# Weighted values of an attention stage: the values as the loaded matrix in column tiles, the transposed weights moving

## The reference, cut to what matters

```python
q, k, v = split_heads(x @ Wq + bq), split_heads(x @ Wk + bk), split_heads(x @ Wv + bv)   # 16 heads of 8
scores = (q k^T + c2p + p2c) / sqrt(24)          # c2p, p2c: relative positions, gathered
probs = softmax(scores, axis=-1)
ctx = einsum('bhqk,bhkd->bhqd', probs, v)        # 128 x 128 weights by 128 x 8 values, per head and batch
out = ctx.reshape(B, S, H) @ Wo + bo + x         # then the layer norm, the outer residual, a second norm
```

## Time and profile before

| | before |
|---|---|
| median of three runs | 2927.15 us |
| profiled execution | 2934.35 us |
| its span | 2932.60 us |
| PE busy | 2580.1 us |
| ACT busy | 2331.3 us |
| DVE busy | 2220.2 us |
| mean granted clock of TensorE | 0.893 of full |

### The profile page before, as it was taken

The page is one execution under the profiler, slowest core; times in us unless marked ns, Lnnn a source line. Parts: engine busy times, 40 slices in busy tenths (PEclk is TensorE's granted clock), DMA queues, the critical chain, the costliest instruction groups (busy, mean ns, idle before and its releaser), DMA issues. The chain is left out here.

```text
span 2932.6 us, 63537 instructions
## 1 busy us (share of the span) xinstructions
PE 2580.1 (88%) x17943; PEld 1570.5 (54%) x17943; DVE 2220.2 (76%) x6591; ACT 2331.3 (79%) x4575; POOL 576.6 (20%) x436
## 2 busy tenths in 40 slices
PE   2999999999999934765669999999999999999997
PEld 1777777777777823652434444444444444444443
DVE  3667767777677657777558888888888888888887
ACT  1778877788788825332779999999999999999997
POOL 2222232222322200113421111111111111111114
PEclk7778978889788855988789999999999999999999
DMA  2000000000000010000011111111111111211113
GB/s 76 13 14 19 11 11 11 16 16 11 11 12 19 2 42 1 0 29 1 0 30 53 47 43 58 43 52 49 43 58 43 52 49 43 58 43 51 50 43 86
DMA packets 182538, 96.02 MB, mean 33 GB/s; under 512 B 22539, under 2 KB 179291, under 8 KB 182491
## 3 DMA queue, kind: packets, MB, share of 16 engines
q1 hardware_dynamic: 182491, 95.45, 11.6%
HBM read 78.10 MB, written 4.73 MB: 28 GB/s over the span
## 5 line engine op out<-in xcount | busy, mean ns | idle before, releaser
L1904 DVE TENSOR_TENSOR c_Hl<-c_HF,c_Hh 128x512 f16<-128x512 f32 x1028 | 679.7, 688 | 160.6 <-ACT c_Hh L1791 144.6
L1787 ACT ACTIVATE c_HF<-c_H,c_b 128x512 f32<-128x512 f32 x1028 | 710.3, 691 | 67.3 <-PE c_H L1726 44.5
L1791 ACT ACTIVATE c_Hh<-c_H,c_b 128x512 f16<-128x512 f32 x1028 | 705.3, 686 | 0.0
L1842 POOL TENSOR_TENSOR c_EX<-c_euler,c_D 128x16 f32<-128x16 f32 x65 | 188.6, 2901 | 1195.8 <-DVE c_D L1877 1195.8
L1726 PE MATMUL c_H<-c_Ch,SH 128*128 128x512 f16 x1028 | 390.0, 379 | 0.0
L1725 PE MATMUL c_H<-c_Cl,SH 128*128 128x512 f16 x1028 | 390.0, 379 | 0.0
L1724 PE MATMUL c_H<-c_Ch,SH 128*128 128x512 f16 x1028 | 390.0, 379 | 0.0
L1735 PE MATMUL c_Y<-c_Hh,SH 128*128 128x512 f16 x1024 | 388.0, 379 | 1.5 <-DVE c_Hl L1904 1.4
L1737 PE MATMUL c_Y<-c_Hl,SH 128*128 128x512 f16 x1024 | 388.1, 379 | 0.0
L1736 PE MATMUL c_Y<-c_Hh,SH 128*128 128x512 f16 x1024 | 388.1, 379 | 0.0
L554 ACT ACTIVATE a_E<-a_T,a_nm 128x128 f32<-128x128 f32 x1024 | 331.0, 417 | 33.0 <-DVE a_nm L642 30.9
(11 more groups left out here) (290 smaller groups left out, 4298.0 us busy)
## 6 DMA issues: line engine op xcount, KB each, us to landing
c_CWB<-c_rows SPq DMA_DIRECT2D x260, 256.0 KB, 4.1
a_QN<-a_QH SPq DMA_DIRECT2D x128, 32.0 KB, 1.8
a_KN<-a_KH SPq DMA_DIRECT2D x128, 32.0 KB, 1.8
out<-d_O SPq DMA_DIRECT2D x16, 256.0 KB, 2.3
a_QN<-a_QL SPq DMA_DIRECT2D x64, 32.0 KB, 1.8
a_KN<-a_KL SPq DMA_DIRECT2D x64, 32.0 KB, 1.8
CUR<-in_ctx SPq DMA_DIRECT2D x1, 1848.0 KB
c_rows<-c_CWR SPq DMA_DIRECT2D x65, 8.0 KB, 1.3
```

Of the source, the lines that this page charges most:

```text
L1787: act.activation(HF[:, k % 4, :], bH[k % 4][:, :], ACT.Gelu_apprx_tanh, bias=b1[:, g % EXPERTS, f:f + 1], scale=1.0 / WSCALE).then_inc(hf_ ...
L1791: act.activation(Hh[:, g % 2, f, :], bH[k % 4][:, :], ACT.Gelu_apprx_tanh, bias=b1[:, g % EXPERTS, f:f + 1], scale=1.0 / WSCALE).then_inc( ...
L1904: dve.tensor_tensor(Hl[:, g % 2, f, :], HF[:, k % 4, :], Hh[:, g % 2, f, :], ALU.subtract)\
```

## The change

The operands of the value product are exchanged. V is stored with 32 columns per head (VCOLS): eight values, a one, and zeros. It is the loaded matrix now, and the 128 queries of ET move. Each of the four heads of a unit writes its own 32 partitions of bO, and the unit its own 128 columns. The result is thus transposed: values on partitions, queries along the row.

To bring it back, ACT copies bO to a new tile OC (`unit_columns`, in steps 7, 11, 15, 19), and PE transposes OC unit by unit (`out_rows`, in steps 9, 13, 17, 21). These transposes go to the two banks bE as well. The banks are handed on by position in one sequence, SLOTS, in which the outputs of a batch come after unit 7, 11, 15 and at the end; slot n uses bank n % 2 and waits (`bank_free`) for the reader of slot n - 2. The steps of the reciprocal move from 7, 11, 15, 19 to 9, 13, 17, 21, those of `out_transpose` and `out_columns` to 10, 14, 18, 22, and those of `out_project` to 11, 15, 19, 23.

```diff
+VCOLS = 32
+def bank_slots():
+    out = []
+    for w in range(UNITS):
+        out.append(("unit", w))
+        if w >= UPB + 3 and w % UPB == 3:
+            out.append(("out", w // UPB - 1))
+    return out + [("out", NB - 1)]
...
-        V = sb("V", [P, NB, NH, DH + 1])
+        V = sb("V", [P, NB, NH, VCOLS])
+        OC = sb("OC", [P, UPB, S])
...
+            const(pool.memset(V[:, :, :, :], 0.0))
...
             def exp_transposes(i, w):
                 pe.wait_ge(e_ok.sem, e_ok.at(i, w + 1))
-                pe.wait_ge(et_ok.sem, et_ok.at(i, w - 1))
+                bank_free(i, slot_of(w))
                 for h in range(HG):
-                    last = pe.transpose(bE[w % 2][:, h * S:(h + 1) * S], E[:, w % 3, h, :], ident[:, :])
+                    last = pe.transpose(bE[slot_of(w) % 2][:, h * S:(h + 1) * S], E[:, w % 3, h, :], ident[:, :])
                 last.then_inc(et_ps.sem, 1)
+            def bank_free(i, slot):
+                kind, k = SLOTS[slot - 2]
+                if kind == "unit":
+                    pe.wait_ge(et_ok.sem, et_ok.at(i, k + 1 if slot >= 2 else 0))
+                else:
+                    pe.wait_ge(on_ok.sem, on_ok.at(i, k + 1 if slot >= 2 else 0))
+            def out_rows(i, b):
+                slot = SLOTS.index(("out", b))
+                pe.wait_ge(oc_ok.sem, oc_ok.at(i, b + 1))
+                bank_free(i, slot)
+                for g in range(UPB):
+                    last = pe.transpose(bE[slot % 2][:, g * S:(g + 1) * S], OC[:, g, :], ident[:, :])
+                last.then_inc(oc_ps.sem, 1)
...
                 if g == 0:
-                    pe.wait_ge(on_ok.sem, on_ok.at(i, b))
+                    pe.wait_ge(oc_ok.sem, oc_ok.at(i, b))
...
                 for h in range(HG):
-                    at = (g * HG + h) * (DH + 1)
-                    last = pe.matmul(bO[:, at:at + DH + 1], ET[:, w % 3, h, :], V[:, b, g * HG + h, :],
-                                     start=True, stop=True)
+                    last = pe.matmul(bO[VCOLS * h:VCOLS * (h + 1), g * S:(g + 1) * S], V[:, b, g * HG + h, :],
+                                     ET[:, w % 3, h, :], start=True, stop=True)
...
-                    if u >= 8 and (u - 8) % UPB == 0:
-                        out_transpose(i, (u - 8) // UPB, last)
-                    if u >= 9 and (u - 9) % UPB == 0:
-                        out_project(i, (u - 9) // UPB)
+                    if u >= 9 and (u - 9) % UPB == 0 and u < 9 + UNITS:
+                        out_rows(i, (u - 9) // UPB)
+                    if u >= 10 and (u - 10) % UPB == 0:
+                        out_transpose(i, (u - 10) // UPB, last)
+                    if u >= 11 and (u - 11) % UPB == 0:
+                        out_project(i, (u - 11) // UPB)
...
+            def unit_columns(i, b):
+                act.wait_ge(pv.sem, pv.at(i, UPB * (b + 1)))
+                act.wait_ge(oc_ps.sem, oc_ps.at(i, b))
+                act.activation(OC[:, :, :].rearrange("p g s -> p (g s)"), bO[:, :], ACT.Copy).then_inc(oc_ok.sem, 1)
...
             def softmax_outputs(i, b):
-                dve.wait_ge(pv.sem, pv.at(i, UPB * (b + 1)))
-                o = bO[:, 0:NH * (DH + 1)].rearrange("p (h e) -> p h e", h=NH)
+                dve.wait_ge(oc_ps.sem, oc_ps.at(i, b + 1))
+                o = bE[SLOTS.index(("out", b)) % 2][:, :].rearrange("p (h e) -> p h e", h=NH)
```

More of the change, by code:

```diff
@@ L41 @@
 C2P_MID, P2C_MID = 47, 17
-CONSTS, TAB, BUILT = 20, 10, 4
+CONSTS, TAB, BUILT = 21, 10, 4
 DVE_CHUNKS = tuple((c, 1) for c in range(1, CHUNKS))
 ACT_CHUNKS = tuple((c, f) for c in range(CHUNKS) for f in range(2) if (c, f) not in DVE_CHUNKS)
+VCOLS = 32
 HALVES = ((0, 0), (0, 1), (1, 0))
@@ L60, in row_x, with slot_of @@
     return ((kind * NG + g) * 2 + j) * NB + b
+def bank_slots():
[5 more added lines that the diff above has]
+    return out + [("out", NB - 1)]
+SLOTS = bank_slots()
+def slot_of(w):
+    return SLOTS.index(("unit", w))
 class Count:
@@ L211, in attention_stage @@
         pv = Count(sem("pv"), UNITS, credit=3)
+        oc_ok = Count(sem("oc_ok"), NB, credit=1)
+        oc_ps = Count(sem("oc_ps"), NB, credit=1)
         rs_ok = Count(sem("rs_ok"), NB)
@@ L455, in _ @@
             pe.sem_inc(pv.sem, pv.credit)
+            pe.sem_inc(oc_ps.sem, oc_ps.credit)
             pe.sem_inc(ot_ps.sem, ot_ps.credit)
@@ L547, in exp_columns @@
                 act.wait_ge(pv.sem, pv.at(i, w - 2))
-                act.activation(ET[:, w % 3, :, :], bE[w % 2][:, :], ACT.Copy).then_inc(et_ok.sem, 1)
+                act.activation(ET[:, w % 3, :, :], bE[slot_of(w) % 2][:, :], ACT.Copy).then_inc(et_ok.sem, 1)
             def exponentials(i, u):
@@ L566, in _ @@
             act.sem_inc(et_ok.sem, et_ok.credit)
+            act.sem_inc(oc_ok.sem, oc_ok.credit)
             x_columns(0, 0)
@@ L588, in body @@
                         exponentials(i, u)
-                    if u >= 8 and (u - 8) % UPB == 0:
-                        out_columns(i, (u - 8) // UPB)
+                    if u >= 7 and (u - 7) % UPB == 0 and u < 7 + UNITS:
+                        unit_columns(i, (u - 7) // UPB)
+                    if u >= 10 and (u - 10) % UPB == 0:
+                        out_columns(i, (u - 10) // UPB)
                     if u >= UNITS and not last:
@@ L808, in body @@
                         add_positions(i, u)
-                    if u >= 7 and (u - 7) % UPB == 0 and (u - 7) // UPB < NB:
-                        softmax_outputs(i, (u - 7) // UPB)
+                    if u >= 9 and (u - 9) % UPB == 0 and (u - 9) // UPB < NB:
+                        softmax_outputs(i, (u - 9) // UPB)
                     if u == 1 and not last:
```

## The result

The changed kernel takes 2961.89 us (median of four runs, 2955.75 to 2969.79) against 2927.91: a ratio of 1.0106, 95% interval 1.0085 to 1.0127. It is slower: by about 31 us by the ratio, by 34 by the two medians, and the interval covers both. The forecast was 2950 us, range 2888 to 3003.

What follows compares the result with a forecast made beforehand. ACT bounds units 6 to 15, PE loop steps 16 to 19. Blocks summed 11 x -0.1 + 4 x 4.9 + 4.5 = +23 us on 2934.35: 2957, or 2950 on the median's footing; range 2888 to 3003.

Steps and rivals of the forecast that it cites:

- ACT binds the units, and a cheaper matmul buys nothing there by itself: Units 6 to 15 at full clock: ACT busy 31.3 of 33.5 us, so ACT binds, not PE.
- Copies on ACT, 0.48 each: unit_columns in steps 7, 11, 15, 19: +0.96 us for 7 and 11, 0.48 each for 15 and 19.
- Step 10: Unit 8's transposes wait for ACT's copy of unit 7, bucket tiles behind them; ACT idles 1.6 us a block.
- Steps 14 and 15: Unit 12 waits for unit 11's copy; exp(15) needs 3.1 against 1.64 us; at full clock chunk 2 comes 1.1 later.
- The step that failed: Pricing of unit_columns on ACT: four copies a block, those in ACT-bound steps 7 and 11 adding 0.96 us.
- X: Time of a unit's eight new value matmuls on PE: 0.74 us at full clock, 1.27 at half.
- Rival (c): Column tiles run in series, 1.06 us at full clock and 1.9 at half; 3017 us; chance 0.08.
- its price of 0.41: X if column tiles work independently, by the skill page's first statement alone; a block some 0.7 us shorter.
- The clock: In ten 62 us blocks and the first, the fall comes as late as in 57 us ones: -0.1 us each.
- rival (b): Clock also holds through steps 20 to 23 and the next block's start: -3.6 us a block, 2896 us; chance 0.22.
- 2.6 + 1.1 = 3.7: Full-clock block up to its chunks: 0.96 for copies plus 1.6 at step 10, and 1.1 for later chunk 2.
- +1.2 was forecast: Steps 19 to 23: ACT's fourth copy, DVE's moved reciprocal and multiply, later PE work; 0.5 to 2.0 us.

Runs made afterwards that it cites:

- experiment 1: Changed kernel with ACT's copy of the results (unit_columns) moved within its step to right behind the transposes' copy: 2919.25 us, ratio 0.9973.
- experiment 8: Changed kernel with the copy of the results on VectorE, behind add_positions of the same step, instead of ScalarE: 2912.89 us, ratio 0.9949.
- experiment 9: Experiment 1's kernel with the norm's last step on DVE in step 11 rather than 9: 2920.69 us, ratio 0.9969.
- experiment 11: Experiment 8's kernel with the norm's last step in step 12 rather than 9: 2902.58 us, ratio 0.9909.
- experiment 7: Experiment 1's kernel with PE's two bucket tiles ahead of the transposes of the exponentials in step 10 alone: 2948.29 us, ratio 1.0067.
- experiment 10: Experiment 9's kernel with PE's bucket tiles ahead of the transposes in step 10: 2902.44 us, ratio 0.9910.
- experiment 6: Changed kernel with all four heads of a unit in one column tile, results of three heads left out: 3029.37 us, ratio 1.0343.
- experiment 5: Experiment 1's kernel with the old form of the value matmuls, transposed weights loaded and 32 columns of V moving: 2972.93 us, ratio 1.0164.
- experiment 4: Changed kernel with only the value matmuls' form undone, transposed weights loaded and 32 columns of V moving: 3150.73 us, ratio 1.0758.

## Why the prediction was right, and where not

The sign and the size came out: +31 us measured, +23 forecast, and 2962 is inside its own range 2920 to 2975. But the sum holds one term too few and others too large, and that these cancel is luck. An estimate: with the 39 us of experiment 1 added, the forecast would have read 2950 + 39 = 2989, so its other terms together were some 27 us too high. I go through them.

*ACT binds the units, and a cheaper matmul buys nothing there by itself.* Right: PE lost 166 us of value matmuls and the kernel did not gain.

*Copies on ACT, 0.48 each.* Right in size (484.95 - 484.47). The prediction charged three of the four in full, 1.44 us a block. Taking them off ACT gave 7 us in experiment 8 and 18 between experiments 9 and 11, which is 0.5 to 1.2 us a block: a little too high.

*Step 10.* 1.49 us of idle ACT measured, 1.6 forecast. The reason given, the transposes' bank, was necessary but not the only one: experiments 7, 9 and 10 show DVE's splits late beside it. The prediction had put the reciprocal's move from step 7 to 9 at nothing there, without a reason; it named the queue of PE behind the wait, not that of DVE.

*Steps 14 and 15.* Before exp(14) and exp(15) ACT is idle 0.67 and 0.72 us for DVE's results in that block, 1.4 against the 3.1 - 1.64 = 1.5 that the prediction had for exp(15). Not tested alone.

*The step that failed.* "unit_columns copies a whole 128x512 bank ... four times a block: steps 7, 11, 15 and 19. Steps 7 and 11 are in the ACT-bound part: +0.96." The copy was priced as work only. It also holds the one bank bO, and the diff's own line, `pe.wait_ge(oc_ok.sem, oc_ok.at(i, b))`, puts the first value matmuls of the next batch behind it. Before, DVE freed this bank with its multiply, and PE's value matmuls of step 8 came just behind it (timelines of DVE and of PE before):

```profile
471.84 0.29 DVE L654 TENSOR_TENSOR a_On<-a_O,a_rs 128x128 f32<-128x128 f32 x1
...
472.21 1.03 PE L435 MATMUL a_O<-a_V,a_ET 128*128 128x9 f32 x8
```

Now ACT does it last in its step 7, at 484.47, when PE has been in step 8 since 481.83. The prediction had this wait at nothing; it is 73.8 us of PE's waiting, and 39 us of the kernel's time by experiment 1.

*X.* Too large: 0.74 at full clock, against 0.35 and 0.13 of entry. I had a head's two passes keep the tiles from running side by side, five intervals of eight; measured, with the change of array shape included, there is no room for that (0.54 alone would be more). Rival (c), tiles in series, is refuted: its 1.06 is near the 0.99 of one tile in experiment 6, not the 0.35 of four. The Trainium skill (TensorEngine Tiling (Array Packing), Key Properties) says that tiles work independently; the runs agree, 0.35 us against 0.99, and its price of 0.41 was the better one.

*The clock.* The forecast had the long fall come at 49 us into every block. No block from 87.68 on has it (the first block still has half clock from 41 to 90 us, as before); what is left are the short falls of 3.4 or 6.8 us, and closing steps and starts such as 508 to 546 ran at full. That is further towards rival (b) than forecast, and the gain at the ends of blocks hid part of the missed wait; how much is not measured apart. By blocks: from opening copy to first chunk 511.77 - 464.30 = 47.47 us, against 494.91 - 453.89 = 41.02 in the 57 us block: +6.45. The forecast had 2.6 + 1.1 = 3.7; the 2.7 left over is what experiment 1 gives for the waits at steps 8, 12 and 16, 39 us over 15 blocks or 2.6. From there to the next scores it is 13.8 against 13.6, +0.2 where +1.2 was forecast; the start 1.3 against 2.3, -1.0. Together +5.6, and the 57 us block has become one of 62.5. The reason that I gave for the clock, the new form, is not shown: experiment 5 has loaded weights again, with 32 columns moving, at 0.97 in the new order. Falls often followed PE standing about 2 us in the units (the changed kernel, experiments 4 and 7), but not always: not in the changed kernel's block that begins at 87.68, after 2.17 us, nor in experiment 6 at 440 to 470, after 1.86. What decides it, and what kept the clock up at the ends of blocks in experiment 5, stays open.

## What to carry to other kernels

An added stage between a producer and its buffer is priced three times: its own time, the moment at which it frees the buffer (the step and place in the list of the engine that does it), and who stands in line behind the one that waits. Where an engine's list is written out by hand, a copy that frees a single bank belongs at the first place where its input is ready. And a wait with two causes shows only the later one: removing either alone gave nothing or a loss here (experiments 7 and 9), removing both gave the gain (experiment 10), so a move that fails is worth a second look for what has become last.

## What the runs showed of the hardware

Four float32 matmuls of 128 moving columns, two passes each, in four column tiles of 32: 0.35 us at full clock. In one tile: 0.99 us, near an estimate of eight passes in series at 0.107 us and 0.13 for the change of shape.

PE standing for about 2 us within the units was followed by half clock in the changed kernel at 485 us, in experiment 4 at 472 and in experiment 7 at 479; in experiment 4, with PE loaded more heavily per unit, it stayed at half for some 20 us, in the changed kernel for 3.4. In the changed kernel's first full block (PE standing 2.17 us up to 107.67) and in experiment 6 (1.86 us up to 441.18) no fall followed. So a wait of 2 us can cost several times its length on PE, and need not.
